# z's half of the input projection at the next turn's start, the output projection in two parts, the next block's statistics earlier

## The reference, cut to what matters

```python
h = _layernorm(x, axis=-1) * (1 + ca) + sa
xz = hidden_states @ in_proj_w.T
x, z = jnp.split(xz, 2, axis=-1)
...
x = jax.nn.silu(jnp.transpose(xc, (0, 2, 1)))       # after the convolution
x_dbl = x @ x_proj_w.T
dt, k, q = jnp.split(x_dbl, [DT_RANK, DT_RANK + D_STATE], axis=-1)
dt = dt @ dt_head_w.T
...                                                  # scan over time gives ys
y = y * jax.nn.silu(z)
out = y @ out_proj_w.T
```

## Time and profile before

| | |
|---|---|
| median of 3 runs | 1822.53 us (1820.58 to 1823.0) |
| the profiled execution | 1821.96 us, span of its instructions 1820.2 us |
| busy share of the span | PE 91%, DVE 81%, POOL 75%, ACT 72% |
| `x_attn` (L1057), one per turn | 16 times, first at 68.8 us, last at 1238.6 us |

### The profile page before, as it was taken

The page is one execution under the profiler, slowest core; times in us unless marked ns, Lnnn a source line. Parts: engine busy times, 40 slices in busy tenths (PEclk is TensorE's granted clock), DMA queues, the critical chain, the costliest instruction groups (busy, mean ns, idle before and its releaser), DMA issues.

```text
span 1820.2 us, 33709 instructions
## 1 busy us (share of the span) xinstructions
PE 1657.9 (91%) x12156; PEld 1424.5 (78%) x12156; DVE 1469.9 (81%) x3084; ACT 1314.7 (72%) x2689; POOL 1369.6 (75%) x644
## 2 busy tenths in 40 slices
PE   6678999999999999999999999997777999999998
PEld 5557788887878888787878878786665888899997
DVE  3548889898988988898898889889897678766663
ACT  3568878888887888878788888876643855666664
POOL 0009899999989999999999999999998343444443
PEclk9899999999999999999999999999997999999999
DMA  5011111212111221221122122112112444455552
GB/s 198 1 56 44 71 66 71 73 68 83 68 68 65 76 83 54 82 76 60 65 76 83 53 83 76 59 61 97 65 70 93 116 128 99 122 139 140 137 136 29
DMA packets 69462, 149.78 MB, mean 82 GB/s; under 512 B 5936, under 2 KB 43312, under 8 KB 68912
## 3 DMA queue, kind: packets, MB, share of 16 engines
q1 hardware_dynamic: 57008, 130.84, 20.7%
q0 software_dynamic: 12288, 16.79, 5.2%
HBM read 121.91 MB, written 17.30 MB: 76 GB/s over the span
## 4 chain that ended last, share of the span: by engine, by line
PE 63%; DVE 14%; ACT 12%; issue 6%; POOL 4%; DMA 0%; DVEq 0%; ACTq 0%; POOLq 0%
PE po L1834 10%; PE ph L1834 9%; DVE room L1179 8%; PE pD L1130 8%; PE pY L1147 7%; PE pA L731 6%; POOL room L1188 3%; PE pB L926 3%; PE pB L936 3%; PE pB L1226 3%; ACT room L1160 2%; PE pA L722 2%; PE pB L957 2%; PE pB L942 2%; PE pA L652 1%
## 5 line engine op out<-in xcount | busy, mean ns | idle before, releaser
L1198 POOL TENSOR_TENSOR room<-room 128x1024 f32<-128x1024 f32 x256 | 608.2, 2376 | 159.4 <-DVE room L1113 139.0
L1179 DVE TENSOR_TENSOR_SCAN room<-pD,last,room 128x256 f32<-128x256 f32 x1024 | 688.7, 731 | 38.3 <-PE pD L1130 26.0
L1188 POOL TENSOR_TENSOR room<-room 128x1024 f32<-128x1024 f32 x256 | 607.8, 2375 | 46.4 <-PE pY L1147 46.2
L1160 ACT ACTIVATE room<-room,kkT 128x512 f32<-128x512 f32 x512 | 359.8, 715 | 57.4 <-PE pD L1130 55.9
L1130 PE MATMUL pD<-fixed,room 128*128 128x128 f32 x2048 | 318.1, 279 | 70.1 <-DVE room L1179 60.5
L1147 PE MATMUL pY<-fixed,room 128*128 128x128 f32 x2048 | 315.6, 277 | 15.1 <-POOL room L1188 15.0
L1130 PEld LDWEIGHTS pD<-fixed,room 128*128 128x128 f32 x2048 | 239.1, 143 | 103.2 <-issue 53.4
L1147 PEld LDWEIGHTS pY<-fixed,room 128*128 128x128 f32 x2048 | 246.2, 144 | 66.8 <-POOL room L1188 30.8
L343 POOL DMA_INDIRECT xg<-xn_rows,W x64 | 67.5, 1055 | 196.5 <-DVE W L337 180.9
L1793 ACT ACTIVATE h<-ph 128x512 f32<-128x512 f32 x128 | 76.6, 598 | 137.9 <-PE ph L1834 101.4
L1834 PE MATMUL po<-w_up,h_up 128*128 128x256 f32 x512 | 149.5, 292 | 3.2 <-DVE h_rest L1701 2.6
(11 more groups left out here) (313 smaller groups left out, 3400.0 us busy)
## 6 DMA issues: line engine op xcount, KB each, us to landing
room<-kq_rows SPq DMA_DIRECT2D x128, 512.0 KB, 3.6
w_in<-w_d SPq DMA_DIRECT2D x32, 1024.0 KB
room<-ndS SPq DMA_DIRECT2D x16, 512.0 KB, 3.2
xt<-x_in SPq DMA_DIRECT2D x16, 256.0 KB, 2.9
y_out<-xo SPq DMA_DIRECT2D x16, 256.0 KB, 2.1
xn_rows<-xnC SPq DMA_DIRECT2D x16, 256.0 KB, 2.2
W<-weights SPq DMA_DIRECT2D x1, 1808.0 KB, 8.8
W<-weights SPq DMA_DIRECT2D x1, 1697.5 KB, 16.4
```

The source lines that it names most:

```text
L1160: act.activation(decT[:, m % 2, t, :], turn2(ndT, it, NT * DI, t * DI, DI), ACT.Copy, bias=1.0, scale=turn2(kkT, it, NT * DS, t * DS + m, ...
L1179: dve.tensor_tensor_scan(run, pD[h][:, k2 * TB:(k2 + 1) * TB], run, last[:, bass.ds(later(it) * (DS * DT) + m * DT + k, 1)], ALU.mult, ALU ...
L1188: pool.tensor_tensor(sq[:, m % 2], st[:, m % 4], kqb[:, m % SLOTS, 1, :].unsqueeze(1).broadcast_to([P, DT, TB]), ALU.mult).then_inc(sem("r ...
L1198: pool.tensor_tensor(st[:, m % 4], turn2(u, it, DT * TB).rearrange("p (k t) -> p k t", k=DT), kqb[:, m % SLOTS, 0, :].unsqueeze(1).broadca ...
```

## The change

z's products and SiLUs go from places 50, 51 (PE) and 46, 52 (ACT) to places 67, 69 and 68, 70, that is 3, 5 and 4, 6 of the next turn, and into bank `pA[1]`; the first waits for `og` there, `low` of the next attention block waits for the last SiLU, and `dt0` waits for no SiLU any more. The output projection becomes `out0` at 25 and `out1` at 28, with `x_scan` at 30 instead of 28. The statistics of the next block of A are made at place 46 of the turn before (`stat_next`), and SP loads the x rows earlier.

```diff
 AT = dict(
-    stat_a=0, ln_a=2, rows_a=4, turn_a=6, mod_a=7, low=8, v=17, lr=14, v_s=17, z=21, abs=21, exl=23, gk=27, G0=27,
+    stat_a=0, stat_next=46, ln_a=2, rows_a=4, turn_a=6, mod_a=7, low=8, v=17, lr=14, v_s=17, z=21, abs=21, exl=23, gk=27, G0=27,
...
-    xs0=45, xs1=46, inz0=50, sz0=46, dkq_mm=50, dkq=52, inz1=51, sz1=52, kturn=53, kk=53, dt0=53, dt1=55, sig0=54,
-    sig1=56, den=57, nd=60, ut=61, u=69, yz0=19, yz1=19, yt0=21, yT0=20, yt1=22, yT1=22, out=25, x_scan=28, ln_d=40,
+    xs0=45, xs1=46, inz0=67, sz0=68, dkq_mm=50, dkq=52, inz1=69, sz1=70, kturn=53, kk=53, dt0=53, dt1=55, sig0=54,
+    sig1=56, den=57, nd=60, ut=61, u=69, yz0=19, yz1=19, yt0=21, yT0=20, yt1=22, yT1=22, out0=25, out1=28, x_scan=30, ln_d=40,
...
             if n == AT["low"]:
                 after(pe, "og", it)
+                if it > 2:
+                    pe.wait_ge(sem("sz"), it * 2 - 2)
...
-            if n == AT["stat_a"]:
+            if (it, n) == (1, AT["stat_a"]) or (it < NB and n == AT["stat_next"]):
+                new = it if n == AT["stat_a"] else it + 1
                 settled(dve)
-                dve.wait_ge(sem("x_in"), (it + 1) * 16)
-                ln_stats(dve, it, "a", lambda t: x_at(it, t))
+                dve.wait_ge(sem("x_in"), (new + 1) * 16)
+                ln_stats(dve, new, "a", lambda t: x_at(new, t))
...
                 if n == AT[f"inz{t}"]:
                     if t == 0:
-                        pe.wait_ge(sem("xs"), it * 2 + 1)
+                        pe.wait_ge(sem("og"), upto(it + 1) + 1)
                     else:
                         pe.wait_ge(sem("sz"), it * 2 + 1)
                     for c in range(DC):
-                        i = pe.matmul(pB[1][:, :], hB[:, c, t * P:(t + 1) * P], inproj[:, c, DI:2 * DI],
+                        i = pe.matmul(pA[1][:, :], hB[:, c, t * P:(t + 1) * P], inproj[:, c, DI:2 * DI],
...
                 if n == AT[f"dt{t}"]:
-                    if t == 0:
-                        pe.wait_ge(sem("sz"), it * 2 + 2)
-                    else:
+                    if t == 1:
                         pe.wait_ge(sem("kk"), it * 3 + 2)
...
-                    act.activation(turn2(szT, it, NT * DI, t * DI, DI), pB[1][:, :], ACT.Silu).then_inc(sem("sz"), 1)
+                    act.activation(turn2(szT, it, NT * DI, t * DI, DI), pA[1][:, :], ACT.Silu).then_inc(sem("sz"), 1)
...
-            if n == AT["out"]:
-                pe.wait_ge(sem("yT"), it * 2 + 2)
-                opf = oproj_g[:, :, :, :].rearrange("p b k n -> p (b k n)")
-                for t in range(NT):
+            for t in range(NT):
+                if n == AT[f"out{t}"]:
+                    pe.wait_ge(sem("yT"), it * 2 + 2)
+                    opf = oproj_g[:, :, :, :].rearrange("p b k n -> p (b k n)")
```

More of the change, by code:

```diff
@@ L82 @@
     inp=DS, dec_t=2 * DS, dec_mm=2 * DS, scanned=DT * DS, saved=DS, read_out=DS, summed=2 * DS, opened=2,
-    yz=2, y_turn=2, yT=2, glast=1, out_mm=1, score_mm=1, scores=1)
+    yz=2, y_turn=2, yT=2, glast=1, out_mm=2, score_mm=1, scores=1)
 PER_BLOCK.update({f"ln{n}_{what}": 1 for n in "abcd" for what in ("rows",)})
@@ L1003, in front_act @@
                     if m == 0:
-                        after(act, "out_mm", it - 1)
+                        after(act, "out_mm", 2 * it - 2)
                     act.wait_ge(sem("in_x"), it * 2 + m + 1)
@@ L1228, in back_pe @@
                                       start=(k == 0), stop=(k == DT - 1))
-                i.then_inc(sem("out_mm"), 1)
+                    i.then_inc(sem("out_mm"), 1)
         def back_act(act, it, n, front):
@@ L1252, in back_dve @@
             if n == AT["x_scan"]:
-                dve.wait_ge(sem("out_mm"), it + 1)
+                dve.wait_ge(sem("out_mm"), 2 * it + 2)
                 dve.wait_ge(sem("x_out"), it * 16)
@@ L1551, in turn_sp @@
                              xo[:, :, :]).then_inc(sem("x_out"), 16)
+            if a is not None and i >= 1 and not (isinstance(i, int) and i + 3 > NB):
+                sp.wait_ge(sem("x_in"), (i + 3) * 16)
+                load(i + 3)
             if s is not None:
@@ L1557, in turn_sp @@
                              xnC[:, :, :]).then_inc(sem("rows_out"), 16)
-            if a is not None and i >= 1 and not (isinstance(i, int) and i + 3 > NB):
-                sp.wait_ge(sem("x_in"), (i + 3) * 16)
-                load(i + 3)
             if s is not None:
```

## The result

| | before | after |
|---|---|---|
| median | 1821.55 us | 1938.99 us (1936.45 to 1940.77) |
| ratio | | 1.0644 (95% interval 1.0625 to 1.0662) |
| span of the profiled execution | 1820.2 us | 1934.7 us |
| `x_attn`, first and last | 68.8, 1238.6 us | 68.5, 1350.4 us |
| mean full turn (13 turns, by `x_attn`) | 79.05 us | 87.25 us |

The change is 117 us slower. Of the 114.5 us that the span gains, the 13 full turns hold 13 x 8.20 = 106.6, turn 1 holds 6.5 (from 74.9 to 81.4) and the stretch behind the last `x_attn` 2.7; the fill before turn 1 is 1.4 shorter.

What follows compares the result with a forecast made beforehand. The turn was taken as PE's queue plus its waits. Terms 4.7 + 1.3 - 1.6 + 0.6 and 1.2 for the clock gave 6.2 us per full turn, 87.6 in all: about 1910 us, range 1866 to 1950.

Steps and rivals of the forecast that it cites:

- the rival of 2071 us: At every table load on ACT, a drain of 1.38 us more, adding 12.4 us a turn; chance 0.01.
- Start to `turn_b`: From `og` to `turn_b`, one unoverlapped chain of z's products, `wo`, SiLU and two loads makes `turn_b` 4.85 us later.
- The clock: Behind PE's wait of 3.6 us before `turn_b`, a half-speed stretch in each turn, costing 1.2 us.
- The middle: From `s_f` to `mod_c`, four loads partly swallowed by waits and slack, plus the projection's second half: +1.3 us.
- this sign: If the turn's middle takes more than 1.3 us, DVE or POOL hold a chain taken as hidden.
- The late part: Up to `kturn`: `xs1` 2.7 us late, then z's absence shortens the way to `kturn`; gives back 1.6 us.
- Statistics: At the turn's start, DVE saves time and PE's 1.04 us wait goes, but PE waits for `og`: no gain.
- `kturn` to `rms` and the other turns: Same ACT chain with DVE's delays, +0.6 us per full turn; turn 1 +4, turn 15 +2, turn 16 +1.
- Loads in ACT's waits: Most loads run while ACT would stand still, only `ln_b`'s remain, 2.57 us a turn: about 1858 us; chance 0.13.
- every load is paid: ACT's queue is the path throughout, so 134 loads add 172 us: about 1994 us; chance 0.08.
- Not slower: ACT's spare time at the turn's start hides the work if `turn_b` is at most +3.4 us: 1804 us; chance 0.03.
- Fewer loads: One load serves Ln and Exp together, `turn_b` at +3.6, about 2.5 us a turn: 1857 us; chance 0.03.

Runs made afterwards that it cites:

- e2: Changed kernel, with the set holding both Ln and Exp asked for behind z's second SiLU (119 loads instead of 221): 1902.76 us, ratio 1.0458.
- e11: Changed kernel, with PE repeating both of z's products, results unread, while it would wait for `turn_b`'s rows: 1918.8 us, ratio 1.0533.
- e1: Kernel before, nothing moved, with only the change's 134 further table loads added at the same places: 1911.48 us, ratio 1.0506.
- e5: Kernel before, with only the output projection in two parts and `x_scan` at 30: 1857.33 us, ratio 1.0209.
- e3: Kernel before, with only z's half moved, with its nine loads per turn: 1912.72 us, ratio 1.0517.
- e6: Kernel before, with only the statistics moved to place 46 and x loaded earlier: 1828.29 us, ratio 1.0052.
- e8: Kernel before, with only z's half moved and one set for Ln and Exp asked for behind the second SiLU: 1854.45 us, ratio 1.0194.
- e9: As e8, with PE repeating one z product, result unread, while it waits for `turn_b`: 1836.55 us, ratio 1.0086 against the kernel before.

## Why the prediction came out as it did

The forecast was 1910 us, the measured time 1938.99: the direction and the range held, and so did the mechanism in the main (the loads on the way to `turn_b`, and the clock behind PE's wait there). The sum was some 29 us short, and the middle of the turn, 13 x 1.49 = 19 of them, had a cause that the forecast did not see. Step by step:

*The loads.* 14 in a full turn, 1283 ns each, ACT at 77.9 busy: as forecast. From the SiLU's end at 742.58 over the load at 742.59 to Ln at 743.89 a switch costs 1.3 us. The Trainium skill, "ScalarE: Activation LUTs", section "What ACT_TABLE_LOAD costs", adds a drain that would make it about 2.66. This trace does not show it, and the rival of 2071 us falls. The Trainium skill, "ScalarE: Activation LUTs", section "Table sets: the hidden batching unit", has one load for ln and then exp. That did not hold for what the build made (45 loads each at L565 and L568); it holds where the set is asked for by name (e2).

*Start to `turn_b`.* Forecast +4.85, measured +5.59. The chain is the one that was written down. It was started at 604.3, while `og` ends at 604.43, and it is longer by a tenth or so at several hand-overs, for instance 1.98 instead of 1.87 from z's second product to its SiLU, and 1.24 instead of 1.1 for `rows_b`.

*The clock.* Forecast +1.2, measured 1.75 (6.96 to `s_f` in the change, 5.21 in e11). The wait of 3.90 did bring the stretch, but in part of the turns it is 6.83 us long, not 3.41. Behind the wait of 1.58 ahead of `dkq_mm` none came; that it could was left to the range.

*The middle.* Forecast +1.3, measured +2.79. This is the term that was wrong: "`x_scan`, two places later, is read by `ln_d` ten places on", with no price. It looked at who reads `x_scan`, and not at what it was moved past on DVE: `x_ffn` with its wait for `wout`. The loads' part was right (+1.43 in e1 against 1.2). The output projection had 0.1, and for a reason that does not hold: its second half stands ahead of `G1` in both kernels. It costs 2.8 in the middle when alone (e5) and about 1.4 on top of the loads (the change against e1 or e3), so the two delays partly hide each other. Both of its costs show in the change: PE waits 1.71 for the scan behind the pile on DVE, and 0.96 ahead of `G0` for ACT, late by its load. In e1 the same load stands there too, but so does the whole projection ahead of `G0`, and PE goes from one to the other without a wait. The text had named this sign: if the middle takes more, DVE or POOL hold a chain taken as hidden. For the larger part it was DVE.

*The late part.* Forecast -1.6 over the two stages, measured +0.99 - 2.78 = -1.8. Its gain at `kturn` is real, and as large as the forecast's 3.0 within 0.2. The +1.4 to `xs1` was a sum of loads and statistics less ACT's wait, and that is not what the runs show: the statistics alone give +0.99 (e6), the loads alone +0.56 (e1), and the change the same +0.99 with norm d's loads as without them (e2, +1.01). That the two stages come so near is in part luck, since the two errors have opposite signs.

*Statistics.* "I book no gain": right, for the reason given (PE then stands before `og`), shown by e6.

*`kturn` to `rms` and the other turns.* +0.2 in place of +0.6 to the next `og`; turn 1 +6.5 in place of +4; the end +2.7 in place of +3.

*The rivals.* "Loads in ACT's waits" and "every load is paid" are both settled by e1: 92.6 us, between the 36 and the 172 that they worked out. "Not slower" needed `turn_b` at +3.4 or less; it stands at +5.59, and with one load (e8) still at +4.2. "Fewer loads", tried in e2, gave 1902.76 and not 1857, since the middle does not go back to its old length (+2.28) and the stretch at half speed stays (+1.42 to `s_f`).

## What to carry to other kernels

A step that brings another function to ACT is priced with all the switches it causes behind it, up to the next place where a set is asked for: here two SiLUs per turn brought nine loads, and beside them the move of the products cost nothing more. A step moved by two places is priced by what it passes in its engine's queue, and by the wait that it used to fill, not only by its reader; and a step cut in two leaves waits open that its whole length had covered. And two delays in one stage do not add: to see what one is worth, take each away alone, and then both.

## What the runs showed of the hardware

The length of a wait of PE alone did not tell whether the clock falls. In e5 PE waits 1.98 us in the middle of 11 full turns; a stretch at 0.50 follows in two of them, and the granted clock stays at 1.00 in the other nine, as it does in the two turns with a wait of 2.33. In e8 it waits 2.53 at the start of all 13, and 12 show a stretch, while in the kernel before a wait of 2.07 was followed by one. What the chip goes by was not settled here. Filling the wait at the start removed the stretch there in all 13 full turns of e9 and of e11; two turns of e11 have one in the middle instead, behind waits of 2.07 and 2.06, and 11 have none.

The load that the build put ahead of an activation did not run in the idle time before it. The load for z's first SiLU starts when the product that the SiLU reads is done (737.64, after an idle time of 0.74 put down to PE's L939), 14.1 us over its 16 times. So a wait of ACT ahead of such a load hid none of it here.
